# A two-network graph kernel: neighbour scores spread over the partitions by DMA, no loop, new orders

## What is computed

```python
h = relu(layernorm(x));  Wh = h @ W
e = leaky_relu(Wh @ a1 [:, None] + Wh @ a2 [None, :])      # 128 x 128 per graph
p = softmax(where(adj > 0, e, -9e15)); p = where(p < 16th highest, 0, p)
x = x + elu(p @ Wh)
h = relu(layernorm(x))
for l in range(3):                                         # the layers l below
    s = leaky_relu((h @ wi[l])[:, None] + (h @ wj[l])[None, :] + b[l])
    agg = softmax(where(mask, s, -inf)) @ h
    y = layernorm(h + agg) * g1[l] + beta1[l]
    ff = gelu(y @ W1[l] + b1[l]) @ W2[l] + b2[l]           # 256 -> 1024 -> 256
    h = layernorm(y + ff) * g2[l] + beta2[l]
out = x + h
```

## Time and profile before

| | |
|---|---|
| median of 3 runs | 2912.39 us (2909.65 to 2912.75) |
| profiled execution | 2917.91 us, of which the span of instructions is 2916.2 us |
| TensorE busy | 95% |
| VectorE, ScalarE, GpSimd busy | 78%, 80%, 71% |
| mean granted TensorE clock | 0.978 of full speed |
| moved by DMA | 89.33 MB |

### The profile page before, as it was taken

One profiled execution on the slowest core, in us unless ns is written; L12 is line 12 of the kernel. 1 busy time (PEld: TensorE's weight loads), 2 busy tenths in 40 slices (PEclk: granted clock), 3 DMA queues, 4 the chain that ended last, 5 costly groups with the idle time before them and its releaser, 6 DMA issues.

```text
span 2916.2 us, 59363 instructions
## 1 busy us (share of the span) xinstructions
PE 2758.3 (95%) x17764; PEld 2462.7 (84%) x17764; DVE 2289.0 (78%) x7766; ACT 2328.4 (80%) x4806; POOL 2080.9 (71%) x2217
## 2 busy tenths in 40 slices
PE   5689999999999999999999999999999999999995
PEld 4578988888988888888888888888898888889884
DVE  6777888888878788788887878788888888887543
ACT  4577888888888788888887878788887888898763
POOL 0356777787777777777777777777777778777774
PEclk9789999999999999999999999999999999999997
DMA  5000011011101101110101111101110111110001
GB/s 177 24 26 27 28 32 34 16 26 34 34 27 34 29 14 34 35 33 27 34 9 34 34 29 32 35 8 34 34 34 27 34 21 24 32 25 18 10 12 15
DMA packets 96384, 89.33 MB, mean 31 GB/s; under 512 B 9120, under 2 KB 94368, under 8 KB 96032
## 3 DMA queue, kind: packets, MB, share of 16 engines
q1 hardware_dynamic: 79136, 68.32, 7.5%
q0 software_dynamic: 16896, 16.78, 4.4%
HBM read 47.34 MB, written 37.75 MB: 29 GB/s over the span
## 4 chain that ended last, share of the span: by engine, by line
PE 50%; DVE 19%; ACT 13%; issue 10%; POOL 6%; DMA 1%; DVEq 0%; ACTq 0%; POOLq 0%; SPq 0%
PE ps_mm L3043 7%; PE ps_mm L3045 7%; PE ps_mm L3044 7%; PE ps_ff L3066 6%; PE ps_ff L3068 6%; PE ps_ff L3067 6%; PE ps_ag L3101 3%; ACT A L1070 2%; DVE junk L2269 2%; PE ps_ht L3113 2%; ACT H L1084 2%; PE ps L3165 2%; ACT a_hi L1078 2%; DVE U L2223 2%; POOL a_lo L507 2%
## 5 line engine op out<-in xcount | busy, mean ns | idle before, releaser
L3066 PE MATMUL ps_ff<-w_hi,a_hi 128*128 128x256 f32 x3072 | 898.3, 292 | 17.0 <-POOL a_lo L507 9.7
L507 POOL TENSOR_TENSOR a_lo<-A,a_hi 128x512 fp32r<-128x512 f32 x384 | 522.6, 1361 | 527.3 <-ACT a_hi L1078 519.6
L3067 PE MATMUL ps_ff<-w_lo,a_hi 128*128 128x256 f32 x3072 | 859.0, 280 | 0.0
L3068 PE MATMUL ps_ff<-w_hi,a_lo 128*128 128x256 f32 x3072 | 858.2, 279 | 0.0
L1070 ACT ACTIVATE A<-ps_mm,b_col 128x512 f32<-128x512 f32 x768 | 518.1, 686 | 308.7 <-PE ps_ff L3068 171.7
L3043 PE MATMUL ps_mm<-ht_hi,w_hi 128*128 128x512 f32 x1536 | 629.0, 410 | 29.0 <-issue 24.1
L3066 PEld LDWEIGHTS ps_ff<-w_hi,a_hi 128*128 128x128 f32 x3072 | 582.4, 190 | 57.9 <-POOL a_lo L507 31.1
L3045 PE MATMUL ps_mm<-ht_lo,w_hi 128*128 128x512 f32 x1536 | 609.0, 396 | 0.0
L3044 PE MATMUL ps_mm<-ht_hi,w_lo 128*128 128x512 f32 x1536 | 606.9, 395 | 0.0
L3067 PEld LDWEIGHTS ps_ff<-w_lo,a_hi 128*128 128x128 f32 x3072 | 583.1, 190 | 13.3
L3068 PEld LDWEIGHTS ps_ff<-w_hi,a_lo 128*128 128x128 f32 x3072 | 582.7, 190 | 0.0
(11 more groups left out here) (120 smaller groups left out, 5349.7 us busy)
## 6 DMA issues: line engine op xcount, KB each, us to landing
xr<-in_x SPq DMA_DIRECT2D x32, 512.0 KB, 4.1
out<-x SPq DMA_DIRECT2D x32, 512.0 KB, 4.5
out<-H POOLq DMA_DIRECT2D x32, 512.0 KB, 6.1
mask_in<-mask_park SPq DMA_DIRECT2D x96, 128.0 KB, 3.6
adj_sb<-in_adj SPq DMA_DIRECT2D x32, 256.0 KB, 4.4
mask_park<-mask_out SPq DMA_DIRECT2D x32, 128.0 KB, 3.7
X<-in_L_gnn_W SPq DMA_DIRECT2D x3, 1024.0 KB, 5.3
H<-in_L_gnn_W SPq DMA_DIRECT2D x3, 1024.0 KB, 6.9
```

Of the source, the lines that this page charges most:

```text
L507: pool.tensor_tensor(a_lo[:, at], A[:, at], a_hi[:, at].bitcast(F32), ALU.subtract).then_inc(s["a_lo_gpsimd"], 1)
L3066: pe.matmul(out_g, a_hi[:, at, cols], w2_hi[:, l, m], start=first, stop=False, skip_group_check=True)
L3067: pe.matmul(out_g, a_hi[:, at, cols], w2_lo[:, l, m], start=False, stop=False, skip_group_check=True)
L3068: last = pe.matmul(out_g, a_lo[:, at, cols], w2_hi[:, l, m], start=False, stop=final, skip_group_check=True)
```

## The change

Three things are changed together.

First, `turn_sj` and `turn_e0` are no longer called (the lists of units that would still use them, TURNED and E0_TURNED, are empty). In their place SP writes the neighbour terms of a unit to device memory, 128 partitions of four values, and reads them back as one row of 512 values broadcast to all partitions. The row lies in pt (or pt0), with the four graphs interleaved, so that a graph's terms are every fourth value:

```diff
+        sj_row = pt[:].rearrange("p (m g) -> p g m", g=G)
+        e0_row = pt0.rearrange("p (m g) -> p g m", g=G)
+        sj_park = nc.dram_tensor("sj_park", [NG, L, P, G], F32, kind="Internal").ap()
+            def park_sj(k, l):
+                sp.wait_ge(s["sij_made"], value(seq(k, l) + 1))
+                sp.dma_start(sj_park[value(k), l], sij[:, l, 1]).then_inc(s_sj_parked[l], 16)
+            def load_sj(k, l):
+                n, before = seq(k, l), parked_before(k, l)
+                sp.wait_ge(s_sj_parked[l], value(before * 16 + 16))
+                if some(n):
+                    sp.wait_ge(s["agg_made"], value(n * 2))
+                sp.dma_start(pt[:], row(sj_park[value(k), l].rearrange("m g -> (m g)"), P * G)).then_inc(s_sj_in[l], 16)
```

park_e0 and load_e0 do the same for e0, with a wait for z_mixed of the group before. `leaky` and `scores_max` read the row in place of the PSUM bank, and node_scores waits until the values before have been parked:

```diff
-                act.wait_ge(s["sj_turned"], value(n + 1))
+                    act.wait_ge(s_sj_in[l], value(parked_before(k, l) * 16 + 16))
...
+                    last = act.activation(U[:, g], ps_s[:, g * P:(g + 1) * P] if turned(k, l) else sj_row[:, g], ACT.Relu,
+                                          bias=sib[:, l, g:g + 1], scale=RISE)
...
+                if some(parked_before(k, l)):
+                    dve.wait_ge(s_sj_parked[l], value(parked_before(k, l) * 16))
```

Second, the loop goes:

```diff
-            with eng.Fori(0, (LAST_STEADY + 1 - FIRST_STEADY) // 2) as j:
-                iteration(At(j, 2, FIRST_STEADY))
-                iteration(At(j, 2, FIRST_STEADY + 1))
+            for i in range(FIRST_STEADY, LAST_STEADY + 1):
+                iteration(i)
```

Third, the lists of steps of all five engines have a new order. Of SP in the steady part:

```diff
             def iteration(i):
-                load_mask(i + 1, 0)
-                load_adj(i + 3)
+                park_sj(i, 1)
                 load_mask(i, 1)
+                load_sj(i, 1)
+                park_sj(i - 1, 2)
+                load_sj(i - 1, 2)
                 load_mask(i - 1, 2)
-                park_mask(i + 2)
-                store_x1(i + 1)
+                load_mask(i + 2, 0)
                 load_x(i + 4)
+                park_sj(i + 2, 0)
+                park_mask(i + 3)
+                load_sj(i + 2, 0)
+                park_e0(i + 3)
+                store_x1(i + 2)
+                load_adj(i + 4)
+                load_e0(i + 3)
```

## The result

The changed kernel takes 3020.94 us in the median (3016.84 to 3027.0), the kernel before beside it 2912.57. The ratio is 1.0375, with an interval of 1.0354 to 1.0395. It is slower by 108 us. The forecast was 2850, with a range to 2895. The profiled execution took 3022.26 us and has a span of 3020.5. One of the four executions of e1_straight, further down, was slow (7572.29 us), and its ratio leaves that one out.

The account below looks back on a forecast made before the run. TensorE was taken as the bound, except at the ends. In span, 2916.2 - 50 (straight code) - 53 (transposes) + 25 (opening) + 10 (tail) + 5 (stalls, strided reads) = 2853, given as 2850 us measured; range 2808 to 2895.

Parts of the forecast that it names:

- The bound: TensorE bounds the kernel in the steady part; at both ends a chain of steps over all engines does.
- Straight code, -50 (24 to 54): In the steady loop, removing ten jumps back on each engine saves 50 us, between 24 and 54.
- Transposes, -53: Taking turn_sj and turn_e0 off TensorE saves 1.78 us an iteration, 53 us over some 30 iterations.
- The trip, 8.1 us, "at nothing" in the steady part: Scores' write and read through device memory take 8.1 us, hidden in the steady part by matmuls of three other units.
- +5 for all stalls and the strided reads: Over the run, stalls such as load_sj waiting for pt, plus reads of every fourth SBUF word, add 5 us.
- SP's queue at nothing: On SP, eight more issues per iteration and the waits ahead of other transfers cost nothing.
- Opening, +25: Before the pipe is full, trips and reordered loads add 25 us, between 0 and 45.
- tail, +10: At the end, the last scores' trip and unit (31, 1) add 10 us, between 3 and 16.
- New orders, up to 45 better: New orders of five engines can't be priced line by line; allowed to gain up to 45 us.
- The buffer `pt` as bound: Rival: in steady iterations, load and hold of pt set the pace, 87 to 94 us an iteration, 2985 to 3200; chance 6%.
- a trip once an iteration by about 1 us: Rival: at unit (i, 1) the trip shows by 1 us in each iteration, total 2880; chance 15%.
- The loop wasn't the jump: Rival: in the loop the jump costs only its own instruction, so the straight-code gain goes, total 2898; chance 5%.

Follow-up runs that it names:

- e1_straight: Also written e1: the kernel before with straight code in place of the hardware loop and nothing else; 2844.4 us, ratio 0.9758.
- e9: The changed kernel with the neighbour scores of all three layers turned on TensorE again, only the end scores through device memory; 2855.08 us.
- e11: The changed kernel with the hardware loop put back, two steady iterations to a round, and nothing else; 3103.32 us, ratio 1.0668.
- e2: The changed kernel, straight and with its new orders, but with turn_sj and turn_e0 back on TensorE, no scores by DMA; 2861.37 us.
- e10: The changed kernel with score rows loaded early from a constant, not waiting for the write, and read with unit stride; results differ; 2815.85 us.
- e4: The changed kernel with load_sj broadcasting a constant row, issued ahead of park_sj without waiting for the write; strided reads kept, results differ; 2839.27 us.
- e12: Like e9, but the neighbour scores of layer 0 alone also go through device memory; 2898.63 us, ratio 0.9948.
- e14: Like e9, but the neighbour scores of layer 2 alone also go through device memory; 2900.81 us, ratio 0.9951.
- e8: The changed kernel with scores written graph by graph in 512 pieces of 4 bytes, so reads are contiguous and results right; 3767.4 us.
- e5: The changed kernel with the other four engines' orders as before; straight code, all scores through device memory, SyncE's list kept; 3601.01 us.

## Why the prediction was wrong, point by point

*The bound.* Right for the kernel before: without the loop (e1) TensorE is idle for 9.8 of the middle's 2334.9 us. It holds in the new orders too as long as no sj goes by DMA: e9's middle has TensorE busy for 2300.79 of 2309.20 us.

*Straight code, -50 (24 to 54).* Right mechanism, too small: in spans 73.9 by e1 and 75.1 by e11, in medians 71 and 82. The step that was off is the comparison of the earlier trace rows: it took `closing` (84.23 us an iteration) as the loop body's speed, but e1 runs the body itself, straight, in 83.4 us (2334.9 / 28; by the marks of the earlier trace rows, 83.3). 86.84 - 83.4 is 3.4 us an iteration, 69 us over the 20 between the marks. The forecast did say that the 52 might hold a difference of order; it looked for it on one side only. Nor does all of the excess sit at the jump, as the prediction had it from the 85.00 us inside a turn: that iteration is 1.8 us slower in the loop too. The branch times of the Trainium skill (Advanced Engine Details and Errata, Control Flow Timing) would give some 2 us, an estimate; e1 and e11 speak against it as a loop's price.

*Transposes, -53.* Borne out, as far as the runs part it from the other way of reading the scores: from e2 to e10 the middle falls by 48.4 us (2318.7 to 2270.3), 1.73 an iteration where 1.78 was forecast. With strided reads (e4) only 30.3 of it are left.

*The trip, 8.1 us, "at nothing" in the steady part, +5 for all stalls and the strided reads.* This is the step that failed. The trip is shorter than forecast, 2.0 + 4.1 = 6.1 us, and still costs 137.6 us in the middle (e9 to the changed kernel). The working counted the distance between units in TensorE's time, "hidden by the matmuls of three other units". In its sum it never asked for the distance in the lists of ScalarE and VectorE between the step that makes the scores and the step that reads them, though it is there that an engine stands, and with it the gelu, ht_high and a_lo of the other three units. The sentence that an engine with idle time costs nothing "unless TensorE waits" was right, and the condition was met in every iteration: turn_h waits 23 times in the 23 iterations of the rows above.
The strided reads are the second half of this step: 19.9 us hidden, 61.7 with the trip in the open, against a bound that put both together at 5. In both numbers is a cost that the forecast had no term for, the long reads of `scores_max` beside GpSimd.

*SP's queue at nothing.* Right: all 96 waits before a read end with the landing of its write, so no read came late for another reason, and all 96 waits before a write end with its sij.

*Opening, +25; tail, +10.* The first mm1 comes at 113.6 us, 25.5 later, and up to (3, 0) it is 29.3. The size was right, its parts weren't, and that is luck: the first mm1 comes at 90.4 us in e1, 105.0 in e2 and 113.6 here, so 14.6 come with the new orders and 8.6 with the trips, where the forecast gave two trips 15. The tail grew by 34.7, three and a half times the term. From e1 to e2 it grows by 18.5 (193.9 to 212.4), with the new orders, which the forecast gave nothing, and from e2 to the changed kernel by 18.3, with the trips.

*New orders, up to 45 better.* In the middle they bring 16.2 us; in all they lose 14.1.

*Rivals.* The buffer `pt` as bound gave 87 us an iteration, which is what came, for a reason that didn't: in the changed kernel no wait before a load is ended by agg, while in e4 93 are, and that kernel is 187.1 us faster. Nor is it "a trip once an iteration by about 1 us": e12 to e14 are this case, at 0.8 to 1.5 us an iteration, but there are three trips, and they add up. "The loop wasn't the jump" fell with e1.

From before to after, in spans: straight code -73.9, new orders +14.1, the way through device memory +164.1, together +104.3.

## What to carry to other kernels

In this kernel a transfer put between a step that makes a value and one that reads it was hidden only where the reader stands, in its own engine's list, further behind the maker than the transfer takes; count that distance in the trace for each reader, not the matmuls that lie between. Where it is too short, the engine stands and everything of other units behind it is late, though ScalarE is busy only 78% of the time. Here straight code alone (e1, 2844.4 us) is the best of the kernels that leave nothing out, and the next is e9 with the one transfer that had its distance.

## What of the hardware was not expected

- A loop's turn back is dear: ten turns cost 71 to 82 us (e1, e11), 7 to 8 us each, of which the waits show 2 to 3 us per engine. For the kernel before, the spans put about half on idle time of TensorE and, by the estimate above, a fifth on the lower clock behind it; the rest is open.
- A write of 2 KB from 128 partitions landed in 2.0 us in 16-byte pieces and 8.2 us in 4-byte pieces (e8). The Trainium skill (DMA: Bandwidth & Descriptors, Anatomy of one DMA, the table of fixed and variable cost) gives the first by its fixed part, and by an estimate from its rule 2.6 us for the broadcast of 256 KB, where 4.1 was measured. Its fit is for DMAs issued from GpSimd; these are SyncE's.
- Reading every fourth word of SBUF took ScalarE 517 in place of 391 ns for 128 values (e4, e10), and VectorE 381 in place of 288 (medians of the reads with no GpSimd step in their way, in the middle of the same two). The Trainium skill (Advanced Engine Details and Errata, Memory Cachelines) says that each access to a new 16-byte line is penalised; the runs agree, and the forecast had passed over it.
- VectorE's `scores_max` (128x128, fp32) took about 1.4 us in place of 0.38 when it read its row from SBUF and started while a GpSimd step of over 1 us ran (39 of 336 in the middle of the changed kernel, 162 of 333 in e5). With the row in PSUM it took 0.26 to 0.29 us each time (before, e9).
